# Turning the rounds of an expert stage: a mixed tile's second products directly ahead of the next mixed tile's first

## The reference

```python
scores = softmax(xf @ w_router)                    # xf: 2048 tokens x 256
expert_weights, expert_indices = top_k(scores, 2)
cw = zeros((T, 8)).at[arange(T)[:, None], expert_indices].add(expert_weights)
h = silu(einsum('td,edh->teh', xf, w1)) * einsum('td,edh->teh', xf, w3)   # hidden 512
y = einsum('teh,ehd->ted', h, w2)
moe_out = einsum('te,ted->td', cw, y)
```

## Time and profile before

| | us |
|---|---|
| median of 3 runs | 707.27 (706.72 to 709.48) |
| profiled execution | 706.14 |
| its span, first to last instruction | 704.3 |
| PE busy | 688.3 (98%) |
| DVE busy | 384.4 (55%) |
| ACT busy | 287.6 (41%) |
| POOL busy | 132.9 (19%) |
| time from one round to the next | 17.31 |

### The profile page before, as it was taken

One profiled execution on the slowest core, in us unless ns is written; L12 is line 12 of the kernel. 1 busy time (PEld: TensorE's weight loads), 2 busy tenths in 40 slices (PEclk: granted clock), 3 DMA queues, 4 the chain that ended last, 5 costly groups with the idle time before them and its releaser, 6 DMA issues.

```text
span 704.3 us, 11180 instructions
## 1 busy us (share of the span) xinstructions
PE 688.3 (98%) x3616; PEld 475.1 (67%) x3617; DVE 384.4 (55%) x951; ACT 287.6 (41%) x599; POOL 132.9 (19%) x111
## 2 busy tenths in 40 slices
PE   8999999999999999999999999999999999999996
PEld 7777777776754444688999746656556777777765
DVE  4688877788724454788777657212333333333331
ACT  3555434543544655766777541110323222222220
POOL 3100000000000000600000104661123334333333
PEclk9999999999999999999999999999999999999999
DMA  9781000000052000004800201423582666666643
GB/s 292 194 250 34 1 0 0 0 0 0 1 167 73 0 5 5 1 1 167 312 0 1 89 2 49 140 86 113 171 222 30 166 153 175 168 164 164 165 101 35
DMA packets 54934, 65.15 MB, mean 92 GB/s; under 512 B 11583, under 2 KB 37905, under 8 KB 54895
## 3 DMA queue, kind: packets, MB, share of 16 engines
q1 hardware_dynamic: 47806, 55.31, 24.6%
q0 software_dynamic: 7088, 9.35, 7.7%
HBM read 48.48 MB, written 16.00 MB: 92 GB/s over the span
## 4 chain that ended last, share of the span: by engine, by line
PE 92%; DVE 3%; ACT 1%; issue 1%; DMA 1%; POOLq 0%; SPq 0%; DVEq 0%; ACTq 0%; POOL 0%
PE ps L567 82%; PE ps L570 10%; DVE stats L1701 1%; DMA early<-in_wk 1%; DVE x_rows L1965 0%; POOLq L133 0%; ACT work L1285 0%; DVE work L1992 0%; DMA work<-expert_rows 0%; DVE x_rows L2001 0%; DVE work L1834 0%; DVE maxes L1832 0%; ACT early L1448 0%; ACT middle L1319 0%; DVE rden L1990 0%
## 5 line engine op out<-in xcount | busy, mean ns | idle before, releaser
L567 PE MATMUL ps<-middle,work 128*128 128x256 f32 (+4 forms) x656 | 177.4, 420 | 1.2 <-ACT work L1285 0.8
L1285 ACT ACTIVATE work<-ps 128x512 f32<-128x512 f32 (+3 forms) x209 | 83.1, 437 | 200.3 <-PE ps L570 183.6
L567 PEld LDWEIGHTS ps<-middle,work 128*128 128x128 f32 (+1 forms) x656 | 115.7, 183 | 48.3 <-issue 29.2
L567 PE MATMUL ps<-late,work 32*128 32x154 f32 (+5 forms) x880 | 141.9, 345 | 0.6 <-ACT work L1285 0.6
L533 POOL DMA_INDIRECT out_rows<-masks x47 | 70.4, 1498 | 152.3 <-DMA out_rows<-masks 56.7
L567 PEld LDWEIGHTS ps<-late,work 128*128 128x128 f32 (+2 forms) x880 | 92.1, 178 | 6.4 <-issue 3.4
L567 PE MATMUL ps<-work,late 128*128 128x256 f32 (+1 forms) x416 | 83.0, 352 | 0.6 <-ACT work L1285 0.5
L570 PE MATMUL ps<-consts_sb,work 128*128 128x128 f32 (+1 forms) x564 | 80.1, 275 | 1.8 <-DVE work L1992 1.2
L499 POOL TENSOR_TENSOR rstd<-var_eps,minus_half 128x8 f32<-128x8 f32 (+1 forms) x10 | 13.9, 1392 | 358.1 <-DVE var_eps L1716 358.1
L570 PEld LDWEIGHTS ps<-consts_sb,work 128*128 128x128 f32 (+1 forms) x564 | 65.1, 140 | 22.0 <-issue 11.6
L567 PE MATMUL ps<-early,late 128*128 128x512 f32 (+2 forms) x192 | 77.6, 608 | 0.3 <-ACT early L1435 0.3
(11 more groups left out here) (226 smaller groups left out, 720.4 us busy)
## 6 DMA issues: line engine op xcount, KB each, us to landing
late<-in_w SPq DMA_DIRECT2D x40, 512.0 KB
early<-in_w SPq DMA_DIRECT2D x16, 512.0 KB, 9.7
expert_rows<-work SPq DMA_DIRECT2D x36, 130.0 KB, 2.9
work<-expert_rows SPq DMA_DIRECT2D x36, 130.0 KB
middle<-in_w SPq DMA_DIRECT2D x8, 512.0 KB, 7.9
out_rows<-x_rows SPq DMA_DIRECT2D x4, 512.0 KB, 3.2
x_rows<-in_x SPq DMA_DIRECT2D x2, 768.0 KB, 10.6
late<-in_ws SPq DMA_DIRECT2D x3, 512.0 KB, 4.0
```

The lines of the kernel that those rows point to most:

```text
L567: return nc.tensor.matmul(o, l, r, start=start, stop=stop, **kw)
L1285: return nc.scalar.activation(o, i, ACT.Copy)
```

## The change

**PE.** A round becomes `pair_up(j)`, `mixed_hidden_t(j)`, `pair_down(j)` u=0, `mixed_trans(j+1)`, `pair_trans(j+1)`, `pair_down(j)` u=1, `mixed_down(j)`, `mixed_up(j+1)`. `mixed_up(0)` moves ahead of the lead's last tiles' second products. `pair_up` and `pair_down` take the quarters in the order 2, 3, 0, 1, and `pair_up` reads three expert numbers in a round instead of two (in the first, four as before; the last `e_step` reads three and not one). The last mixed tile's `mixed_hidden_t(7)` stands between the quarters of `pair_up(7)`, its `mixed_down(7)` ahead of `pair_down(7)`, and `pair_trans(8)` between the two halves of `pair_down(7)`. The waits follow the new order; new ones are that of `pair_trans` for all of the previous pair's products by DVE (bank 1) and that of `mixed_up` for ACT's copy out of bank 1.
**ACT** runs the w2 copy and the mixed tile's silu ahead of the pair's four, **DVE** the previous mixed tile's scaling and this one's product ahead of the pair's, and the slots' metadata (`metas`) behind the mixed tile's copy. **SP** waits for the mixed tile's weight buffer ahead of the pair's. **POOL** adds the last mixed tile ahead of pair 7.

```diff
+PAIR_ORDER = (2, 3, 0, 1)
 # SP
             for j in range(1, ROUNDS):
                 next_pair(j)
                 round_rows(j)
+                round_second(j, 2 * LEAD + 2 * j)
                 pair_weights(j)
-                round_second(j, 2 * LEAD + 2 * j)
 # POOL
+            for j in range(ROUNDS - 1):
+                pair(j, adds(LEAD) + 64 * j)
+                mixed(j, adds(LEAD) + 64 * j + 32)
+            mixed(ROUNDS - 1, adds(LEAD) + 64 * (ROUNDS - 1))
+            pair(ROUNDS - 1, adds(LEAD) + 64 * (ROUNDS - 1) + 32)
+            pair(ROUNDS, adds(LEAD) + 64 * ROUNDS)
 # PE, pair_trans
                 pe.wait_ge(q["d_ld"], 32 * j + 32)
+                after(pe, q["d_hh"], 4 * j)
 # PE, pair_up
-                for f in range(FC):
-                    if isinstance(j, int) and j == 0:
-                        pe.wait_ge(q["e_hh"], LEAD - 1 + f // 2)
+                for n, f in enumerate(PAIR_ORDER):
+                    if f < 2 and isinstance(j, int) and j == ROUNDS:
+                        pe.wait_ge(q["d_hh"], 4 * j)
                     elif f < 2:
-                        pe.wait_ge(q["e_hh"], LEAD + j)
+                        pe.wait_ge(q["e_hh"], LEAD + j + 1)
+                    elif isinstance(j, int) and j == 0:
+                        pe.wait_ge(q["e_hh"], LEAD)
                     else:
                         pe.wait_ge(q["d_yc"], 2 * j + f - 3)
...
+                    if n == 1 and between is not None:
+                        between()
 # PE, pair_down
-                            pe.wait_ge(q["d_hh"], 4 * j + max(f + 1, 3))
+                            pe.wait_ge(q["d_hh"], 4 * j + max(n + 1, 2))
 # PE, mixed_up
+                pe.wait_ge(q["d_xt"], j + 1)
                 for w in range(2):
-                    pe.wait_ge(q["d_hh"], 4 * j + w + 1)
+                    if isinstance(j, int) and j == 0:
+                        pe.wait_ge(q["e_hh"], LEAD - 1)
+                    else:
+                        pe.wait_ge(q["d_hh"], 4 * j + w - 1)
 # PE, the order
-            def round_(j, more=True):
-                e2, e1 = pair_up(j, (2 * j, ONE + WHOLE + j))
-                mixed_up(j, e1)
+            def round_rest(j, e2, e1, e_next):
+                mixed_hidden_t(j)
                 pair_down(j, e2, (0,))
-                mixed_hidden_t(j)
+                mixed_trans(j + 1)
+                pair_trans(j + 1)
                 pair_down(j, e2, (1,))
-                if more:
-                    mixed_trans(j + 1)
-                pair_trans(j + 1)
                 mixed_down(j, e1)
+                mixed_up(j + 1, e_next)
+            def round_(j):
+                round_rest(j, *pair_up(j, (2 * j, ONE + WHOLE + j, ONE + WHOLE + j + 1)))
...
+            e1, e8 = e_step(LEAD - 1, (ONE + WHOLE, slot_of(LEAD - 2)))
+            mixed_up(0, e1)
+            e_down(LEAD - 2, e8)
             e_hidden_t(0, LEAD - 1)
+            e2, e1, e_next, e9 = pair_up(0, (0, ONE + WHOLE, ONE + WHOLE + 1, slot_of(LEAD - 1)))
             e_down(LEAD - 1, e9)
+            round_rest(0, e2, e1, e_next)
             with pe.Fori(1, ROUNDS - 1) as j:
                 round_(j)
+            e2, e1, e_last = pair_up(ROUNDS - 1, (2 * ROUNDS - 2, ONE + WHOLE + ROUNDS - 1, 2 * ROUNDS),
+                                     lambda: mixed_hidden_t(ROUNDS - 1))
+            mixed_down(ROUNDS - 1, e1)
+            pair_down(ROUNDS - 1, e2, (0,))
+            pair_trans(ROUNDS)
+            pair_down(ROUNDS - 1, e2, (1,))
+            pair_up(ROUNDS, ())
+            pair_down(ROUNDS, e_last)
 # ACT
-            def round_(j, more=True):
-                pair_silu(j)
+            def round_(j):
                 act.wait_ge(q["e_y"], LEAD + j)
                 second_w2(0, ONE + WHOLE + j)
                 mixed_silu(j)
+                pair_silu(j)
                 mixed_ht(j)
-                if more:
-                    mixed_xt(j + 1)
+                mixed_xt(j + 1)
                 pair_xt(j + 1)
 # DVE
+            def round_(j, buf):
+                mixed_y(j - 1, 1 - buf)
+                mixed_hh(j)
                 pair_hh(j)
-                metas(j + 1, more)
-                mixed_hh(j)
-                pair_yo(j, (0,))
                 mixed_ht(j)
-                pair_yo(j, (1,))
-                mixed_y(j, buf)
+                metas(j + 1)
+                pair_yo(j)
...
+            mixed_y(last, last % 2)
+            metas(ROUNDS, False)
+            pair_yo(last)
             pair_hh(ROUNDS)
             pair_yo(ROUNDS)
```

More of the change, by code:

```diff
@@ L550, in _, with pair @@
                     accumulate(to[n % 4][:, 0:1], yo[n % 4])
-            for j in range(DOUBLES):
+            def pair(j, done):
                 pool.drain()
-                pool.wait_ge(q["e_add"], adds(LEAD) + 64 * j)
+                pool.wait_ge(q["e_add"], done)
                 for u in range(2):
@@ L1128, in e_up @@
                     last.then_inc(q["e_h"], 1)
-                    if w == 0 and lagging is not None:
-                        lagging = expert_of(slot_of(lagging))
-                return lagging
+                    if w == 0:
+                        experts = [expert_of(n) for n in slots]
+                return experts
             def e_hidden_t(i, k):
@@ L1155, in e_down, with e_step @@
                 last.then_inc(q["e_y"], 1)
-            def e_step(n):
-                e = e_up(n // 2, n % 2, n - 2)
+            def e_step(n, slots=()):
+                e, *rest = e_up(n // 2, n % 2, (slot_of(n - 2),) + slots)
                 e_hidden_t(n // 2, n % 2 - 1)
@@ L1163, in e_step @@
                 e_down(n - 2, e)
+                return rest
             def pair_trans(j):
                 pe.wait_ge(q["d_ld"], 32 * j + 32)
+                after(pe, q["d_hh"], 4 * j)
                 after(pe, q["d_xt"], j)
@@ L1261, in _ @@
             e_hidden_t(0, 0)
-            for n in range(2, LEAD):
+            for n in range(2, LEAD - 1):
                 e_step(n)
-            e8, e2, e1, e9 = pair_up(0, (slot_of(LEAD - 2), 0, ONE + WHOLE, slot_of(LEAD - 1)))
+            e1, e8 = e_step(LEAD - 1, (ONE + WHOLE, slot_of(LEAD - 2)))
+            mixed_up(0, e1)
+            e_down(LEAD - 2, e8)
             e_hidden_t(0, LEAD - 1)
-            e_down(LEAD - 2, e8)
-            mixed_up(0, e1)
+            e2, e1, e_next, e9 = pair_up(0, (0, ONE + WHOLE, ONE + WHOLE + 1, slot_of(LEAD - 1)))
             e_down(LEAD - 1, e9)
[L1269 to L1274, removed]
+            round_rest(0, e2, e1, e_next)
             with pe.Fori(1, ROUNDS - 1) as j:
                 round_(j)
-            round_(ROUNDS - 1, more=False)
-            e, = pair_up(ROUNDS, (2 * ROUNDS,))
-            pair_down(ROUNDS, e)
+            e2, e1, e_last = pair_up(ROUNDS - 1, (2 * ROUNDS - 2, ONE + WHOLE + ROUNDS - 1, 2 * ROUNDS),
[6 more added lines that the diff above has]
+            pair_down(ROUNDS, e_last)
         @block.scalar
@@ L1684, in _ @@
             mixed_silu(0)
+            e_ht(0, LEAD - 1)
+            pair_silu(0)
             mixed_ht(0)
@@ L1689, in _ @@
                 round_(j)
-            round_(ROUNDS - 1, more=False)
+            act.wait_ge(q["e_y"], LEAD + ROUNDS - 1)
+            second_w2(0, ONE + WHOLE + ROUNDS - 1)
+            mixed_silu(ROUNDS - 1)
+            pair_silu(ROUNDS - 1, (0, 1))
+            mixed_ht(ROUNDS - 1)
+            pair_silu(ROUNDS - 1, (2, 3))
+            pair_xt(ROUNDS)
             pair_silu(ROUNDS)
@@ L2277, in e_step, with pair_hh @@
                 e_y(n - 2)
[L2279 to L2282, removed]
+            def pair_hh(j, turns=range(FC)):
+                for n in turns:
+                    f = PAIR_ORDER[n]
+                    dve.wait_ge(q["d_h"], 4 * j + n + 1)
+                    dve.wait_ge(q["d_sil"], 4 * j + n + 1)
                     after(dve, q["d_y"], 2 * j)
@@ L2289, in pair_yo @@
                         dve.wait_ge(q["e_add"], adds(EARLY + 4))
+                    elif u == 0 and isinstance(j, int) and j == ROUNDS:
+                        dve.wait_ge(q["e_add"], 64 * j + adds(LEAD))
                     elif u == 0:
@@ L2308, in mixed_y @@
             def mixed_y(j, buf):
[L2309 to L2312, removed]
+                dve.wait_ge(q["e_add"], 64 * j + (adds(LEAD) - 64))
                 meta = to_rows(ONE + WHOLE + j, buf, True)
@@ L2350, in _ @@
                 round_(2 * i + 2, 0)
-            round_(ROUNDS - 1, (ROUNDS - 1) % 2, more=False)
+            last = ROUNDS - 1
+            mixed_y(last - 1, (last - 1) % 2)
+            mixed_hh(last)
+            pair_hh(last, (0, 1))
+            mixed_ht(last)
+            pair_hh(last, (2, 3))
+            mixed_y(last, last % 2)
+            metas(ROUNDS, False)
+            pair_yo(last)
             pair_hh(ROUNDS)
```

47 lines of the change are left out of this document (22 added, 25 removed).

## The result

| | before | changed |
|---|---|---|
| median of 11 runs, us | 707.27 | 704.54 |
| lowest, us | 705.75 | 704.28 |
| profiled execution, us | 706.14 | 707.8 |
| its span, us | 704.3 | 705.9 |
| round, us | 17.31 | 16.97 |

The forecast was 705.8, 1.3 above the measured median. One of the eleven runs of the kernel before took 2497.05 us, which the median doesn't feel. The same kernel measured twice more gave 0.9984 (0.9968 to 1.0001) and 0.9981 (0.9965 to 0.9997).

A forecast was written before the change was run, and what follows sets the result against it. PE, busy for 688.3 of 704.3 us, was taken to bound the kernel. Visits -2.4, register loads -0.2 and the end +1.1 gave -1.5 us, from 707.27 to 705.8, with a range of 703.4 to 708.8.

The forecast's parts named there:

- Fewer visits: PE in the rounds: seven visits fewer to the 64 columns at 0.35 us each, seam free, -2.4 us.
- Rival C: Seam between mixed blocks costs as much as the two edges it removes: +0.9 us, 708.2; chance 0.10.
- Register loads: PE's expert-number reads: first pair's 0.3 us back, 0.1 lost in `e_step(9)`, third read in rounds free: -0.2 us.
- Rival D: Third register load empties PE's queue, 0.3 us in seven rounds: together +0.6 us, 707.9; chance 0.08.
- The hand-over: From `pair_up` to `pair_down`: 1.73 us of PE work covers the last quarter's product, needing 1.10 us; cost 0.
- Rival E: Last quarter's product comes one turn late, PE waits 1.1 us in eight rounds: +7.3 us, 714.6; chance 0.08.
- Pair 8's weights: Fetch ahead of `pair_up(8)`: at most 5.1 us needed, 6.0 available, 0.9 us left; cost 0.
- POOL in the round: POOL's adds take 14.2 us against a round of 17.0 after the change, so they stay hidden.
- The end: From the start of `pair_down(8)`: 11.4 us against 10.3, from adding the mixed tile ahead of pair 7; +1.1 us.
- The sum: Whole kernel: -2.4 - 0.2 + 1.1 = -1.5 us, median 705.8; chance 0.62.
- rival B: The end costs nothing more, adds land sooner and only PE's 2.6 us count: 704.7; chance 0.12.

The follow-up runs named there:

- x2: Changed kernel with the pair's second half product put between `mixed_down(j)` and `mixed_up(j+1)`, j = 0 to 6; ratio 1.0021 to the kernel before.
- x7: Changed kernel with five expert numbers read in `pair_up` in rounds 1 to 6 instead of three; ratio 0.9952 to the kernel before.
- x1: Changed kernel with the last mixed tile's second products and adds put back behind pair 7; ratio 0.9959 to the kernel before.
- x3: Changed kernel with the last mixed tile's rows not added to the output; ratio 0.9935 to the kernel before.
- x9: The same kernel as x1, run and profiled once more; ratio 0.9955 to the kernel before.
- x10: The kernel of x1 without POOL's drain ahead of pairs 7 and 8; ratio 0.9956 to the kernel before.
- x4: Changed kernel with pair 8's rows scaled into the mixed tiles' two buffers; ratio 0.9960 to the kernel before.

## Why the prediction was right, point by point

**Fewer visits, -2.4.** Right in mechanism and size, and shown by x2. The round was to be 16.96 us and is 16.96 to 16.97; 7 x 0.346 = 2.4 (0.346 is half of the 0.69 in a round). The seam costs a step, nothing more, and x2 puts the whole gain back. Rival C is out. The Trainium skill's rule (TensorEngine Tiling (Array Packing), Key Properties), that it is the change of mode that drains and not the change of tile, agrees at the seam (0.21 us) and at the two edges of x2.

**Register loads, -0.2.** The first pair's 32 passes take 560.17 - 553.26 = 6.91 us, so its 0.3 is back; PE's 2.72 less the 2.42 of the visits leaves 0.3 in all, so the lead's last step lost nothing where I gave 0.1: -0.3. The third read in the rounds is free, as taken, but with more room than the sum showed, which let the two reads start as long before `pair_up` as in the old order and so had 0.35 us left. TensorE's register loads of one round in the changed kernel:

```profile
L1112 PEldq TENSOR_LOAD <-slot_expert x3: 294/432/602, 620.2 to 621.9; - x3
L1112 PEldq SEQ_ASSERT  x3: 18/18/18, 620.9 to 622.7; - x3
```

They start 2.5 us ahead of `pair_up` (622.75), where before they started 0.8 ahead, and are over at 622.7, some 1.5 us before the next instructions are due. The likely reason, not tested, is that with `mixed_up` at the end of the loop more of PE's time is queued when the loop turns. Rival D is out by the round of 16.96 and by x7.

**The hand-over, 0.** Right. `pair_down` waits for DVE's product of the last quarter, and shows no stall: in the round above its u=0 takes 631.92 - 630.19 = 1.73, the steady 8 passes. At pair 7 DVE ends that product at 682.18 (681.76 + 0.42), before `pair_down(7)` begins at 683.06. Rival E is out.

**Pair 8's weights, 0.** Right: in the changed kernel `pair_down(7)` u=1 takes 687.06 - 685.33 = 1.73 and `pair_up(8)` 693.97 - 687.06 = 6.91, both the steady passes without a gap. Only x2 loses 0.17 there.

**POOL in the round, hidden.** Right in all profiles of the changed kernel, but the 14.2 us were too short a measure. They were taken from the quiet end, and x1's first profile shows 18.6 for a round whose adds fall together with weight fetches (the DMA engines move up to 406 GB/s there, from 594 to 599 us). In that execution, with the last mixed tile behind its pair, the chain fell behind the rounds and stayed behind to the end.

**The end, +1.1.** The mechanism is right in the main: a DMA instead of PE releases DVE, x3 shows that the adds hold the end, and x9 that the third part of the change costs 0.6 to 1.1 us of it. The sum put the whole 1.1 on that part; x9's 10.8 us, without it, are still 0.5 above the 10.3 of the one profile of before. The end was to take 11.4 us and took 11.9, 11.7 and 11.4. Against the 10.3 that is +1.6, +1.4 and +1.1; by the spans at full clock it is 0.1 to 0.9, so the price of the end against the kernel before is not settled.
The 11.4 were hit by terms that cancel. The mixed tile's first add comes 0.76 us after DVE's start on its rows (683.18 to 683.94) and not the 0.48 + 0.8 I put there: -0.5. The step from its second half to pair 7 was taken at 4.12 from the earlier trace rows and measured 5.7, 5.3 and 5.0: +0.9 to +1.6. The others were mostly a little too long and give back 0.3 to 0.5 together: in the first profile 3.34 for 3.44, 1.88 for 2.07, 5.09 for 5.2 and 5.97 for 6.1 from the last pair's first add to the end.

**The sum, -1.5.** By the profiles -1.1, -1.3 and -1.6, by the runs -2.7, -1.1 and -1.3 (the ratios 0.9962, 0.9984 and 0.9981 of 707.3). The sets of runs differ in how often they meet the lower clock told of below: by their mean clocks 1 execution of 11 in the first, 7 of 12 in each of the others. At full clock the spans, 705.2 to 705.4 before and 702.7, 703.4 and 702.9 after, give -1.8 to -2.6, about a microsecond more than the profiles, which is what the quick profile of before lacks. So the -1.5 is met by the profiles, where it was worked out, and is likely too small for the typical execution; rival B, an end that costs nothing, would give -2.6, and its 704.7 is nearer to the first median than the forecast is. The traces refute B's mechanism, an end that PE sets, but not its number. That the sum agrees with the profiles as well as it does is in part luck, since it was built on the same quick execution and its terms at the end cancel.

**What stays open.** Why the mixed tile's second half lands late. DMA by the microsecond behind its issue at 687.28 (last columns clock, DMA share, GB/s):

```profile
689.00:690.00 1.00, 1.00 (x6) 0.89 (x5) 0.42 (x1) 0.37 (x1) 0.00 (x0) 1.00 0.61 78
690.00:691.00 1.00, 1.00 (x7) 0.87 (x6) 0.00 (x0) 0.29 (x1) 0.00 (x0) 1.00 0.03 3
691.00:692.00 1.00, 1.00 (x6) 0.90 (x5) 0.42 (x1) 0.10 (x1) 0.00 (x0) 1.00 0.02 1
```

Most of it moves by 690, and a few last packets come behind 691. It was so, more or less, in all nine profiles with this order and this add (steps of 5.0 to 5.7, or 4.3 to 4.8 without the drain), and not with the tile behind its pair (4.1 to 4.2, or 3.4 without the drain). One more thing divides them: in each of the nine a single packet of some 16 KB on the queue for instructions (q8) falls between the second half's start and pair 7's first add, and in the last step of x1, x9, x10 and the kernel before none does. That is a coincidence in time; no run here tells whether it is the cause.

## What to carry to other kernels

Where PE is the bound, look at the distances between starts and not only at its busy time: 4% of a round here lay at the edges between full-width and half-width matmuls, and ordering equal widths together took half of that away with the same work. Before counting a gain of PE, follow the last outputs through every serial chain behind it: a reordering that gains on PE can lose part of it there, and the last steps are worth trying in both orders. Where runs of one kernel scatter by more than the effect, set the traces against a common instruction ahead of the change, and take more than one trace of the kernel before: here one quick execution of it makes the change look about a microsecond worse.

## What the runs showed of the hardware

TensorE's granted clock differs between executions of the same code ahead of the change. The stretch from 260 to 300 us, the same code in all kernels, in the changed kernel's first and second profile (last columns the granted clock, DMA share, GB/s):

```profile
260.00:300.00 40.00, 37.90 (x168) 19.61 (x166) 25.11 (x50) 23.26 (x42) 12.03 (x10) 0.91 0.03 4
```

```profile
260.00:300.00 40.00, 37.90 (x197) 20.69 (x196) 25.82 (x53) 24.98 (x45) 12.10 (x10) 1.00 0.03 4
```

Two microseconds at a time, the first one reads:

```profile
284.00:286.00 2.00, 1.33 (x10) 0.74 (x9) 1.97 (x6) 1.89 (x4) 0.00 (x0) 1.00 0.00 0
286.00:288.00 2.00, 1.44 (x20) 1.27 (x23) 0.74 (x6) 1.47 (x4) 1.11 (x2) 0.95 0.00 0
288.00:290.00 2.00, 1.48 (x15) 0.77 (x8) 1.27 (x2) 0.38 (x1) 2.00 (x2) 0.50 0.00 0
...
294.00:296.00 2.00, 2.00 (x21) 0.90 (x20) 0.19 (x1) 0.07 (x1) 1.92 (x3) 0.84 0.00 0
```

The granted clock falls to 0.50 (1.2 instead of 2.4 GHz) for about 7 us, behind some 4 us in which PE was busy for 2.8, and comes back behind a stretch in which it was fully busy. In the second profile it stays at 1.00 although PE is as busy, over the 40 us and, 2.8 of 4 us, from 284 to 288. In the five profiles with 0.91 (changed, x2, x3, x4, x7) the common point comes at 509.4 to 510.1 us, in the others at 507.0 to 507.9. What decides between the two, no run here shows. It moves a run by as much as the change does, and explains why sets of 11 or 12 runs of one kernel had medians of 704.5, 706.1 and 706.6. The clock is at 0.50 too in the last 1.3 to 6.8 us of every span, behind PE's last instruction.

A drain of POOL ahead of a pair lengthens the step to that pair's add by 0.8 us beyond the landing that is waited for anyway (4.16 against 3.38 in x9 and x10; 5.0 to 5.7 against 4.3 to 4.8 in the changed order), of which 0.5 to 0.6 reach the end of the span. Two adds of a pair are issued 1.87 us apart; the halves of a tile, which wait for each other, 3.4 in quiet and 4.9 to 5.3 beside a weight fetch (x1).
